# Two attention hops of a graph network: a new order of the steps of each round, three landing places, fewer idle products

## What is computed

```python
def agg(x):
    a_input = jnp.concatenate([x[head], x[tail]], axis=-1)
    e = jnp.sum((a_input @ fc_w.T + fc_b) * rel_e, axis=-1)
    e = jnp.where(e > 0, e, 0.2 * e)
    m = jax.ops.segment_max(e, head, num_segments=N)
    ex = jnp.exp(e - jax.lax.stop_gradient(m)[head])
    denom = jax.ops.segment_sum(ex, head, num_segments=N)
    w = ex / denom[head]
    agg_emb = jax.ops.segment_sum(x[tail] * w[:, None], head, num_segments=N)
    return agg_emb + x
for _ in range(n_hops):                                  # n_hops = 2
    x = agg(x)
    norm = jnp.maximum(jnp.linalg.norm(x, axis=-1, keepdims=True), 1e-12)
    x = x / norm
x = _layernorm(x_before + x, axis=-1)                    # behind the second hop
```

## Time and profile before

| | us |
|---|---|
| median of 3 runs | 6409.13 (6401.49 to 6412.13) |
| the profiled execution, its own time | 6410.99 |
| its span | 6409.2 |
| first hop (`l2a`), from 3578 to 4451 | 873 |
| second hop (`l2b`), from 4451 to 5357 | 906 |
| PE busy in the span | 5644.9 (88%) |
| DVE / ACT / POOL busy | 4652.7 / 4457.7 / 3534.5 |

### The profile page before, as it was taken

How to read it: one execution, slowest core, us unless ns; L and a number is a source line. 1 busy time by engine, 2 the same in 40 slices (tenths; PEclk the granted TensorE clock), 3 DMA queues, 4 the chain that set the end, 5 groups by cost and what they waited for, 6 DMA issues and landing times. The chain is left out here.

```text
span 6409.2 us, 146244 instructions
## 1 busy us (share of the span) xinstructions
PE 5644.9 (88%) x32700; PEld 4709.4 (73%) x32701; DVE 4652.7 (73%) x16722; ACT 4457.7 (70%) x15208; POOL 3534.5 (55%) x3365
## 2 busy tenths in 40 slices
PE   6537999987799999899999899997888887999999
PEld 2326999976677777699999677775666666888888
DVE  9986999987655552377777555555777776988898
ACT  1966999982244442288888577775999995777777
POOL 0776777757666667744444454444455554444444
PEclk9668999998899999999999899998999998999999
DMA  1045777768666666677777677776788874444443
GB/s 50 3 8 167 214 212 211 211 210 251 205 193 194 196 190 201 184 221 222 223 222 221 180 219 217 215 218 176 240 248 251 252 234 129 127 125 127 127 126 119
DMA packets 1164323, 1175.57 MB, mean 183 GB/s; under 512 B 307118, under 2 KB 1038421, under 8 KB 1163282
## 3 DMA queue, kind: packets, MB, share of 16 engines
q1 hardware_dynamic: 1012692, 956.04, 49.1%
q0 software_dynamic: 151360, 216.47, 13.6%
HBM read 963.01 MB, written 393.59 MB: 212 GB/s over the span
## 5 line engine op out<-in xcount | busy, mean ns | idle before, releaser
L215 POOL DMA_INDIRECT landing_first<-messages,by_dst_meta x768 | 826.4, 1076 | 665.2 <-PE l1b_ps_b L1578 368.2
L215 POOL DMA_INDIRECT landing_last<-x,by_dst_meta x384 | 434.9, 1133 | 569.4 <-PE l_ps_a L1715 484.9
L2022 POOL DMA_INDIRECT landing_last<-z,by_src_meta x408 | 425.4, 1043 | 433.3 <-PE l2b_ps_g L2272 309.0
L2022 POOL DMA_INDIRECT landing_last<-x,by_src_meta x408 | 409.9, 1005 | 405.9 <-PE l2a_ps_g L2272 243.1
L215 POOL DMA_INDIRECT landing_first<-in_x,by_src_meta x384 | 404.7, 1054 | 187.4 <-PE l_ps_a L1010 119.3
L1532 ACT ACTIVATE l1a_x_t<-l1a_ps_x,by_dst_first 128x256 f32<-128x256 f32 x400 | 168.0, 471 | 398.0 <-PE l1a_ps_x L1564 398.0
L1576 PE MATMUL l1b_ps_b<-root,l1b_x_t 128*128 128x256 f32 x1600 | 425.9, 389 | 0.0
L1576 PE MATMUL l1a_ps_b<-root,l1a_x_t 128*128 128x256 f32 x1584 | 416.4, 385 | 2.8 <-issue 1.3
L1020 PE MATMUL l_ps_b<-l_w,l_both 128*128 128x256 f32 x1624 | 418.0, 380 | 0.0
L1023 PE MATMUL l_ps_b<-l_w,l_agg_t 128*128 128x256 f32 x1624 | 416.8, 379 | 0.0
L1734 PE MATMUL l_ps_b<-l_w,l_mix_t 128*128 128x256 f32 x1592 | 396.5, 392 | 9.9 <-DVE l_mix_t L1651 9.8
(11 more groups left out here) (418 smaller groups left out, 18172.0 us busy)
## 6 DMA issues: line engine op xcount, KB each, us to landing
l_both<-in_x_both SPq DMA_DIRECT2D x416, 256.0 KB
z<-l2a_result SPq DMA_DIRECT2D x400, 152.0 KB
x<-l1b_result SPq DMA_DIRECT2D x392, 152.0 KB, 3.2
l2a_x<-x SPq DMA_DIRECT2D x48, 1216.0 KB
l1b_x<-h SPq DMA_DIRECT2D x408, 128.0 KB
l1b_res<-x SPq DMA_DIRECT2D x408, 128.0 KB
l1a_x<-x SPq DMA_DIRECT2D x404, 128.0 KB
l_x<-x SPq DMA_DIRECT2D x402, 128.0 KB, 2.3
```

What stands on the lines that cost most here:

```text
L215: pool.indirect_dma_start(gathered[:, slot, 0:D], None, source[0:count, :], bass.IndirectOffsetOnAxis(ap=rows, axis=0), bounds_check=limit ...
L2022: pool.indirect_dma_start(gathered[:, k, :], None, x_in[0:N_NODES, :], bass.IndirectOffsetOnAxis(ap=rows, axis=0), bounds_check=limit, oob ...
```

## The change

The parts, of which all but the landing places concern the order or the place of work:

1. First hop, inverse root and scaling a round later: ACT `guess` and `scale_rows`, DVE `have_square`, `square`, `weigh` and `improve` go from octet n+1 to octet n.
2. Other orders of the steps on DVE, ACT and PE in both hops. In the second hop `measure` stands in one piece, both guesses follow it, `apply` stands ahead of `take_chances`, and PE does all four parts of `aggregate` ahead of `spread`.
3. `gathered` holds three octets (LANDINGS = 3) in the fixed octets; the last, general ones still use two places.
4. Second hop: three of eight rows are scaled and shifted by DVE (`scale_some`, SCALED_BY_DVE = 3), five stay with ACT; SP waits for them on two semaphores.
5. Idle products: none in the first hop; four in the second, behind the second `turn_chances`.
6. To make room, `squares` is BF16 and `restart` covers only the general octets.

```diff
+LATER = -(-MAX_ITEMS // RING) * RING + 3 * RING - OCTETS_FIXED * OCT
+LANDINGS = 3
...
         self.dynamic = not isinstance(self.number, int)
+        self.landing = self.half
+        self.landings = self.lap + (1 - HOPS_FIXED + OCTETS_FIXED // LANDINGS)
         self.general = general if self.dynamic else self.number >= OCTETS_FIXED
         assert self.general is not None
+        if not self.general and not self.dynamic:
+            self.landing, self.landings = self.number % LANDINGS, self.number // LANDINGS + 1
+        self.landed_at = slice(self.landing * OCT, (self.landing + 1) * OCT)
...
-        gathered = landing.slots(HOP, ROW)
+        gathered = landing.slots(LANDINGS * OCT, ROW)
...
-        squares = ph.sb("squares", [P, OCT, D], F32)
-        restart = ph.sb("restart", [P, ITEMS], F32)
+        squares = ph.sb("squares", [P, OCT, D], BF16)
+        restart = ph.sb("restart", [P, LATER], F32)
...
                     for q in range(OCT):
                         k = octet.base + q
-                        sp.wait_ge(s["out_ready"], octet.item + (q + 2))
+                        if last_hop and q < SCALED_BY_DVE:
+                            sp.wait_ge(s["scaled"], octet.number * SCALED_BY_DVE + (q + 1))
+                        elif last_hop:
+                            sp.wait_ge(s["out_ready"], octet.number * (OCT - SCALED_BY_DVE) + (q - SCALED_BY_DVE + 2))
+                        else:
+                            sp.wait_ge(s["out_ready"], octet.item + (q + 2))
                         sp.dma_start(x_out[bass.ds(rows[q], P), :], result[:, k, :]).then_inc(s["stored"][k], 16)
...
                 if not last_hop:
-                    for half in range(2):
-                        pool.memset(gathered[:, half * OCT:(half + 1) * OCT, :], 0.0).then_inc(s["g_zeroed"], 1)
-                    pool.wait_ge(s["g_zeroed"], 2)
+                    for n in range(LANDINGS):
+                        pool.memset(gathered[:, n * OCT:(n + 1) * OCT, :], 0.0).then_inc(s["g_zeroed"], 1)
+                    pool.wait_ge(s["g_zeroed"], LANDINGS)
...
                 def wait_free(octet, h):
-                    if octet.after(2):
-                        pool.wait_ge(s["agg_done"], octet.item + (h * 4 + 4 - 2 * OCT))
+                    places = 2 if octet.general else LANDINGS
+                    if octet.after(places):
+                        pool.wait_ge(s["agg_done"], octet.item + (h * 4 + 4 - places * OCT))
...
-                        pass_wait(dve, s, in_g[o.half * 2 + h], (o.lap + 1) * 64)
+                        pass_wait(dve, s, in_g[o.landing * 2 + h], o.landings * 64)
...
+                def scale_some(o):
+                    o.wait(dve, norm.shifted)
+                    for j, k in o.each()[:SCALED_BY_DVE]:
+                        dve.tensor_scalar(result[:, k, :], result[:, k, :], inv2.root[:, k:k + 1], norm.bias[:, k:k + 1], ALU.mult, ALU.add)\
+                            .then_inc(s["scaled"], 1)
...
                 if last_hop:
-                    steps = [(add_residual, 0), (centre, 0), (scores, 2), (guard, 1), (part(add_self, 0), 1), (part(add_up, 0), 1),
-                             (have_variance, 0), (maximum, 2), (part(add_self, 1), 1), (part(add_up, 1), 1), (find_nodes, 3),
-                             (have_square, 1), (lambda o: inv2.square(dve, o), 0), (lambda o: inv2.weigh(dve, o), 0),
-                             (lambda o: inv2.improve(dve, o), 0), (square, 1), (weigh, 1), (shift_bias, 0), (improve, 1)]
+                    steps = [(add_residual, 0), (guard, 1), (centre, 0), (scores, 2),
+                             (part(add_self, 0), 1), (part(add_up, 0), 1), (part(add_self, 1), 1), (part(add_up, 1), 1),
+                             (have_variance, 0), (find_nodes, 3), (maximum, 2), (have_square, 1),
+                             (lambda o: inv2.square(dve, o), 0), (lambda o: inv2.weigh(dve, o), 0),
+                             (lambda o: inv2.improve(dve, o), 0), (square, 1), (shift_bias, 0), (weigh, 1), (improve, 1),
+                             (scale_some, 0)]
                 else:
-                    steps = [(find_nodes, 3), (scores, 2), (guard, 1), (part(add_self, 0), 1), (part(add_up, 0), 1), (maximum, 2),
-                             (part(add_self, 1), 1), (part(add_up, 1), 1), (have_square, 1), (square, 1), (weigh, 1), (improve, 1)]
+                    steps = [(guard, 1), (find_nodes, 3), (scores, 2), (have_square, 0),
+                             (part(add_self, 0), 1), (part(add_up, 0), 1), (maximum, 2),
+                             (part(add_self, 1), 1), (part(add_up, 1), 1), (square, 0), (weigh, 0), (improve, 0)]
...
-                    for j, k in o.each():
+                    for j, k in o.each()[SCALED_BY_DVE:]:
...
                 if last_hop:
-                    steps = [(lambda o: norm.square(act, o, result), 0), (lambda o: measure(o, 0, 4), 1), (lambda o: inv2.guess(act, w.shift, o), 0),
-                             (part(chances, 0), 2), (part(chances, 1), 2), (lambda o: measure(o, 4, 4), 1), (decay, 2),
-                             (lambda o: inv.guess(act, w.shift, o), 1), (part(take_chances, 0), 2), (part(take_chances, 1), 2), (apply, 0)]
+                    steps = [(lambda o: norm.square(act, o, result), 0), (lambda o: measure(o, 0, 4), 1),
+                             (lambda o: measure(o, 4, 4), 1), (lambda o: inv2.guess(act, w.shift, o), 0),
+                             (lambda o: inv.guess(act, w.shift, o), 1), (part(chances, 0), 2), (part(chances, 1), 2), (decay, 2),
+                             (apply, 0), (part(take_chances, 0), 2), (part(take_chances, 1), 2)]
                 else:
-                    steps = [(lambda o: measure(o, 0, 3), 1), (part(chances, 0), 2), (part(chances, 1), 2), (decay, 2),
-                             (part(take_chances, 0), 2), (lambda o: measure(o, 3, 5), 1), (part(take_chances, 1), 2),
-                             (lambda o: inv.guess(act, w.shift, o), 1), (part(scale_rows, 0), 1), (part(scale_rows, 1), 1)]
+                    steps = [(lambda o: inv.guess(act, w.shift, o), 0), (lambda o: measure(o, 0, 3), 1), (part(chances, 0), 2),
+                             (part(chances, 1), 2), (decay, 2), (part(take_chances, 0), 2), (lambda o: measure(o, 3, 5), 1),
+                             (part(take_chances, 1), 2), (part(scale_rows, 0), 0), (part(scale_rows, 1), 0)]
...
-                        pe.wait_ge(in_g[o.half * 2 + n // 2], (o.lap + 1) * 64)
+                        pe.wait_ge(in_g[o.landing * 2 + n // 2], o.landings * 64)
...
-                def fill_early(o, n):
-                    if o.after(1):
-                        pe.wait_ge(s["mixed"], o.item - 1)
-                    keep_busy(pe, c, ps_g[:, 4, 0:TILES + 1], n)
-
-                def fill_late(o, n):
-                    pe.wait_ge(s["mixed"], o.item + 3)
-                    keep_busy(pe, c, ps_g[:, 0, 0:TILES + 1], n)
-
                 if last_hop:
-                    steps = [(part(aggregate, 0), 1), (part(aggregate, 1), 1), (part(aggregate, 2), 1), (spread, 2), (part(aggregate, 3), 1),
-                             (part(fill, 16), 2), (part(turn_chances, 0), 2), (look_up, 3), (part(fill, 4), 2),
-                             (part(turn_chances, 1), 2), (part(fill, 4), 2)]
+                    steps = [(part(aggregate, 0), 1), (part(aggregate, 1), 1), (part(aggregate, 2), 1), (part(aggregate, 3), 1),
+                             (spread, 2), (part(turn_chances, 0), 2), (look_up, 3), (part(turn_chances, 1), 2),
+                             (part(fill, 4), 2)]
                 else:
-                    steps = [(part(aggregate, 0), 1), (part(aggregate, 1), 1), (part(fill_early, 4), 1), (spread, 2),
-                             (part(aggregate, 2), 1), (part(aggregate, 3), 1), (part(fill_late, 20), 1), (part(turn_chances, 0), 2),
-                             (part(fill_late, 4), 1), (part(turn_chances, 1), 2), (look_up, 3), (part(fill_late, 6), 1)]
+                    steps = [(part(aggregate, 0), 1), (part(aggregate, 1), 1), (spread, 2), (part(aggregate, 2), 1),
+                             (part(aggregate, 3), 1), (part(turn_chances, 0), 2), (look_up, 3), (part(turn_chances, 1), 2)]
```

34 lines of the change are left out of this document (21 added, 13 removed).

## The result

| | before | after |
|---|---|---|
| median | 6406.83 us (6401.49 to 6412.13, 4 runs) | 6299.45 us (6293.82 to 6303.15, 4 runs) |
| ratio | | 0.9832, 95% interval 0.9815 to 0.9849 |
| span of the profiled execution | 6409.2 | 6298.3 |
| granted clock in the windows of the two hops | 0.99 and 0.93 | 0.87 and 0.74 |

The changed kernel is 107 us faster. The forecast was 24 us faster, 6385, with a range of 6240 to 6455: the side was right, the size between four and five times too small.

The account below looks back on a forecast made before the run. It took the first hop as a ring of waits and the second as bound by ACT. -108 for the first hop, +82 for the second and +2 once gave -24; 6387, less 1.9 for the median: 6385 us, range 6240 to 6455.

Parts of the forecast that it names:

- the ring: First hop: one closed chain of waits through ACT and DVE sets the octet's period, 12.7 us against 16.1.
- DVE's added wait: First hop: DVE waits to overwrite `z` until the octet two before is scaled; the eight scalings take 3.6 us.
- First hop, the clock: PE idles about 3.1 us before the first turn; two of three octets slow at 14.6, average 14.0 us, -108 us.
- the sum of 18.3: Second hop: period per octet with PE as the bound; less 0.1 it is 18.2 against 16.6, +82 us.
- the end of the second turn: Second hop: counted from the first chance, turn, look-up and turn at half clock end at 7.6 us.
- surcharge for the late clock: Second hop: 1.1 us on top of 3.5 for sixteen aggregates, as full clock does not come back at once.
- the forecast allowed 0.1: Second hop: 0.1 us taken off the period because some turns begin ahead of the clock's fall.
- The forecast's residual: Second hop, SP's queue: the load starts some 4 us later but has 9 us until DVE wants it; cost nothing.
- a sign of being wrong: The prediction called itself wrong if DVE waits for gathers or the residual; no size given.
- The third landing place: Gathered rows: zeroing costs +2.3 us once; it removes 0.6 us per octet of gather waits, already left out.
- The rivals: Full clock: first hop keeps it (12.7 per octet, 6320 us, chance 0.13); second regains it before second turn (15.4, 6242, 0.15).
- Scalings on DVE: Second hop: three `scale_some` on DVE at 0.33 us each, hidden; ACT has 1.5 us less.

Follow-up runs that it names:

- root_back: Changed kernel with the first hop's inverse root and scaling back at octet n+1, no idle products there; 6368.7 us, ratio 0.9944 to the kernel before.
- the run that shows it: Changed kernel with, in the second hop, twenty idle products ahead of the first turn and four on each side of the look-up; 6256.7 us.
- two_places: Changed kernel with two landing places for gathered rows instead of three; 6550.8 us, ratio 1.0238 to the kernel before.
- all_three: Changed kernel with idle products added in both hops, first hop's look-up behind the second turn, second hop's residual load one round earlier ahead of the store; 6149.5 us.

## Why the prediction was right on the side and wrong in size

**First hop, the ring.** Summed at 12.7 us; the fast octets took 12.39. The step holds term by term (the octet with the maximum at 4021.16): first chance to first copy 2.8, copy and squares 2.5, second copy 0.5, scaling until `add_self` starts 3.8 with DVE's added wait at the place named, 1.3 from there to the maximum and 1.55 to the next chance, 12.4 in all. root_back gives the counter-proof: its ring, summed the same way at 13.9, was 13.88.

**First hop, the clock.** Mis-sized: "I take half of these as slow, and every octet after a fast one", two of three slow at 14.6. Measured: an octet after a fast one slow but for two, none after a slow one, and a slow one 14.02 on average, since the fall often comes only inside the look-up or behind it. (23 x 14.02 + 24 x 12.36) / 47 = 13.17, not 14.0. The gain was 137, not 108; the forecast's "between 13.4 and 14.6" did not reach it.

**Second hop.** The mechanism was right, PE and not ACT the bound, clock 0.74, look-up 3.45 + 0.85 us. The term that was mis-sized is the period: the sum of 18.3 was too long by 0.9 in the slow octet shown. Up to the end of the second turn 7.46 (7.6), idle products 1.10 (1.3), aggregates 4.30 (4.6), last rows of `add_self` 1.02 (1.0), variance and `find_nodes` 1.45 (1.7), maximum to the next chance 2.06 (2.1), 17.39 in all. Laid behind each other in the ring, all terms but the last rows of `add_self` came out up to 0.3 shorter than they were summed; the largest is the aggregates', whose surcharge for the late clock was 0.8 and not 1.1. In the rows the end of one instruction overlaps the start of the next, which the sum of durations left out. Beside that, 18 of the 47 fixed octets keep their clock through the first turn and take 16.0 to 17.1, mostly 16.4 to 16.6; the forecast allowed 0.1 for them. The cost was 32 us, not 82. This was the largest error: 50 of the 86 us between forecast and measurement, against 29 in the first hop; of the rest 2 are the zeroing and most the last layer's, which is chance.

**The forecast's residual.** "the next residual's load thus starts some 4 us later than now but has 9 us until DVE wants it, so nothing": it came to nothing only because PE was slower. The prediction had named a wait for the residual as a sign of being wrong, and it came: DVE waited up to 4.0 us for it in the window of the changed kernel, the load took 8.5 us of flight in the run that shows it, and with the clock kept it became what the hop stood on.

**The third landing place.** Priced at +2.3 for its zeroing, with 0.6 us of waits that the sum "already leaves out". For the sum that was right, the ring assumed gathers in time; the zeroing was not to be seen. But it was the one part on which the others stand: without it, two_places lies at 6551. The prediction gave this part no more than its 0.6 us of waits, and wrote no sum for the ring that it opens.

**The rivals.** Full clock was reached by the change itself in neither hop. all_three shows where it would have led: 12.47 and 14.64 per octet, against 12.7 and 15.4 in the rivals' sums.

**Scalings on DVE.** 0.35 us each, forecast 0.33, hidden, and worth nothing while PE is the bound.

**What was luck.** The 24 us forecast were the difference of two terms that were off by 29 and 50 us. Both had been put too slow; had both been off as far the other way, the change would have come out some 55 us slower than the kernel before. That the size lay inside the range rests on the width of the range.
